# Third convolution tap by an accumulating transfer, and the absolute maximum of four tiles at once on VectorE

## What is computed

```python
def bit_linear(x, w):                       # act_quant: 127 / absmax of a token's row; weight_quant: -1, 0, 1 times a scale
    xq = x + stop_gradient(act_quant(x) - x)
    wq = w + stop_gradient(weight_quant(w) - w)
    return einsum('bsd,hd->bsh', xq, wq)

h = bit_linear(x, w1)                       # 1024 -> 4096
h = depthwise_conv1d(h, conv_w, conv_b)     # three taps along the tokens, padding 1
h = silu(h)
y = bit_linear(h, w2)                       # 4096 -> 1024; needs the absmax of every token over all 4096 rows of h
x = x + layernorm(y)
```

## Time and profile before

| | us |
|---|---|
| median of 3 runs (lowest, highest) | 1610.01 (1600.94, 1643.06) |
| the profiled execution | 1595.02 |
| its span, slowest core (core 3) | 1593.5 |
| spans of the 8 cores | 1575.8 to 1593.5 |
| window 0, from its first scaled copy to the transpose of the maximum | 981.7 to 1099.2 |
| windows 1, 2, 3, the same | 1121.5 to 1225.0; 1257.3 to 1360.0; 1393.0 to 1497.2 |

### The profile page before, as it was taken

The page is one execution under the profiler, slowest core; times in us unless marked ns, Lnnn a source line. Parts: engine busy times, 40 slices in busy tenths (PEclk is TensorE's granted clock), DMA queues, the critical chain, the costliest instruction groups (busy, mean ns, idle before and its releaser), DMA issues.

```text
span 1593.5 us, 23415 instructions; the slowest of 8 cores (1575.8 to 1593.5 us)
## 1 busy us (share of the span) xinstructions
PE 1278.4 (80%) x8148; PEld 794.3 (50%) x8148; DVE 888.0 (56%) x1449; ACT 830.2 (52%) x1118; POOL 94.6 (6%) x165
## 2 busy tenths in 40 slices
PE   2686898798995997988989965653898899799887
...
GB/s 277 194 161 106 179 234 200 188 230 233 172 84 170 154 107 178 153 168 138 187 142 149 146 238 149 166 151 64 1 15 59 61 1 54 41 41 28 27 67 66
DMA packets 86961, 206.31 MB, mean 129 GB/s; under 512 B 8471, under 2 KB 50759, under 8 KB 82668
## 3 DMA queue, kind: packets, MB, share of 16 engines
...
q1 hardware_dynamic: 60620, 91.02, 19.4%
...
HBM read 170.99 MB, written 33.79 MB: 129 GB/s over the span
## 4 chain that ended last, share of the span: by engine, by line
PE 47%; DVE 15%; DMA 13%; issue 11%; ACT 11%; SPq 3%; DVEq 0%; ACTq 0%; POOLq 0%
PE psum L740 11%; PE psum L899 10%; PE psum L863 10%; DMA b_gz<-s_sz 4%; PE psum L653 4%; PE psum L700 4%; DMA f_xr<-x_rev_t 2%; PE psum L800 2%; DMA f_wr<-w_in_t 2%; DMA b_wcb<-w_t 2%; DVE b_h L1357 2%; PE psum L772 2%; DVE b_ev L1309 1%; DVE f_xt L1225 1%; DVE f_xl L1232 1%
## 5 line engine op out<-in xcount | busy, mean ns | idle before, releaser
L863 PE MATMUL psum<-b_xq,b_w1q 128*128 128x257 f16 x2048 | 260.2, 282 | 91.3 <-DVE b_ev L1309 82.6
L863 PEld LDWEIGHTS psum<-b_xq,b_w1q 128*128 128x128 fp8e4 x2048 | 202.2, 101 | 155.2 <-issue 112.9
L899 PE MATMUL psum<-b_w2q,b_hq 128*128 128x512 fp8e4 x1024 | 243.4, 388 | 7.7 <-DVE b_x2t L1394 7.7
L899 PEld LDWEIGHTS psum<-b_w2q,b_hq 128*128 128x128 f16 x1024 | 102.4, 100 | 115.6 <-issue 18.2
L1629 ACT ACTIVATE b_hs<-b_hs,c_cw 128x512 f32<-128x512 f32 x128 | 92.0, 719 | 57.6 <-DVE b_hs L1317 57.5
L1271 DVE SCALAR_TENSOR_TENSOR b_y<-psum,c_dsb,b_gz 128x256 f32<-128x256 f32 (+1 forms) x64 | 30.8, 482 | 147.4 <-PE psum L740 73.0
L1314 DVE SCALAR_TENSOR_TENSOR b_hs<-b_ev,c_cw,b_hs 128x512 f32<-128x512 f32 x128 | 95.1, 743 | 20.6 <-ACT b_hs L1625 20.5
L1317 DVE SCALAR_TENSOR_TENSOR b_hs<-b_ev,c_cw,b_hs 128x512 f32<-128x512 f32 x128 | 96.1, 751 | 14.4 <-DVE b_hs L1314 1.4
L1625 ACT ACTIVATE b_hs<-b_ev,c_cw 128x512 f32<-128x512 f32 x128 | 90.3, 707 | 13.2 <-DVE b_ev L1309 13.2
L1587 ACT ACTIVATE b_yh<-b_y 128x256 bf16<-128x256 f32 (+1 forms) x64 | 26.2, 410 | 129.3 <-DVE b_y L1271 118.0
L1309 DVE TENSOR_TENSOR b_ev<-psum,b_rbc 128x514 f32<-128x514 f32 x128 | 87.4, 685 | 1.0 <-PE psum L863 1.0
...
## 6 DMA issues: line engine op xcount, KB each, us to landing
f_xr<-x_rev_t POOLq DMA_DIRECT2D x15, 2048.0 KB, 11.3
f_pk<-w_t POOLq DMA_DIRECT2D x16, 1024.0 KB, 7.6
b_wca<-w_t POOLq DMA_DIRECT2D x32, 512.0 KB, 4.4
b_wcb<-w_t POOLq DMA_DIRECT2D x32, 512.0 KB, 6.0
b_wck<-w_t POOLq DMA_DIRECT2D x16, 1024.0 KB, 5.0
...
f_lab<-s_logat SPq DMA_DIRECT2D x16, 512.0 KB, 6.5
```

What stands on the lines that cost most here:

```text
L863: e.matmul(psum[:, o:o + 257], sb_w1q.ap()[:, k * DH + mh * 128:k * DH + mh * 128 + 128], x[:, c:c + 257], start=k == 0, stop=k == KD - 1) ...
L899: e.matmul(ps[4 + (t % 2) * 2 + half], sb_hq[i].ap()[:, kh * 128:kh * 128 + 128], sb_w2q.ap()[:, kh * D + half * 512:kh * D + half * 512 + ...
```

## The change

- On most tiles the third tap no longer is a VectorE instruction. ScalarE writes the product of the shifted slot and the third weight to one of two slots of a new buffer `sb_t2` (`tap2`), and GpSimd's queue issues a transfer of that slot, 128 partitions by 2048 bytes (256 KB), that adds it to the tile in `sb_hs` (`accum_op=ALU.add`). `tap_by_dma` says on which: in windows 1 to 3 all tiles below 29, in window 0 the odd ones below 29 (14 of 32).
- A slot of `sb_t2` is used again when the transfer of two users earlier has landed (`TAP`). The scaled copy of a tile waits for `tap2` and the second tap of three tiles earlier, since it overwrites their slot of `sb_ev`.
- SiLU of tile m comes in the loop's step m + 3 and no longer in m + 1, and waits for the transfer, or for `conv`. The last four tiles close up.
- The absolute values on ScalarE (L1637) and the two-tile maxima (L1331) go. VectorE reduces four tiles at once with `tensor_reduce` (maximum of absolute values; the reduced axis steps from tile to tile, 2048 bytes), at g = 8, 12, ... 32, then two tiles at g = 33 and two at g = 34, and takes the maximum with the 512 running columns after each but the first.
- The loads of the second weight matrix move into a loop with the tap transfers on GpSimd's queue.

```diff
+    def tap_by_dma(w, mh):
+        return mh < KH - 3 and (w > 0 or mh % 2 == 1)
...
+                if w or g > 2:
+                    pw, pm = divmod(w * KH + g - 3, KH)
+                    if tap_by_dma(pw, pm):
+                        e.wait_ge(*F_A.at("tap2", pw, pm))
+                    e.wait_ge(*F_V.at("tap1" if tap_by_dma(pw, pm) else "conv", pw, pm))
                 e.tensor_tensor(ev_of(w, g), psum[:, b * 512 + 255:b * 512 + 255 + WX], sb_rbc.ap(), op=ALU.mult
                                 ).then_inc(*F_V.up("ev", w, g))
...
-                                       op0=ALU.mult, op1=ALU.add).then_inc(*F_V.up())
-                e.wait_ge(*F_V.last())
-                e.scalar_tensor_tensor(hs_of(m), x[:, 2:2 + WT], cwb[:, m * 3 + 2:m * 3 + 3], hs_of(m),
-                                       op0=ALU.mult, op1=ALU.add).then_inc(*F_V.up("conv", w, m))
-            if g >= 4 and g % 2 == 0:
-                m = g - 4
-                v_acc(e, w, m)
-        v_acc(e, w, KH - 2)
+                                       op0=ALU.mult, op1=ALU.add).then_inc(*F_V.up("tap1", w, m))
+                if not tap_by_dma(w, m):
+                    e.wait_ge(*F_V.last())
+                    e.scalar_tensor_tensor(hs_of(m), x[:, 2:2 + WT], cwb[:, m * 3 + 2:m * 3 + 3], hs_of(m),
+                                           op0=ALU.mult, op1=ALU.add).then_inc(*F_V.up("conv", w, m))
+            if g >= 8 and g % 4 == 0:
+                v_absmax(e, w, g - 8, 4)
+            if g > KH:
+                v_absmax(e, w, KH - 4 + (g - KH - 1) * 2, 2)
+
+    def v_absmax(e, w, m, n):
+        acc, new = sb_acc.ap()[:, 0:WT], sb_acc.ap()[:, WT:2 * WT]
+        e.wait_ge(*F_A.at("silu", w, m + n - 1))
         if m:
             e.wait_ge(*F_V.last())
-            e.tensor_tensor(sb_acc.ap(), sb_acc.ap(), sb_abs.ap(), op=ALU.max).then_inc(*F_V.up("max", w, m))
+        e.tensor_reduce(new if m else acc, caps(sb_hs, m * WT, [[KH * WT, 128], [1, WT], [WT, n]]), axis=AXX, op=ALU.max,
+                        apply_absolute_value=True).then_inc(*F_V.up())
+        if m:
+            e.wait_ge(*F_V.last())
+            e.tensor_tensor(acc, acc, new, op=ALU.max).then_inc(*F_V.up("acc", w))
...
+                if tap_by_dma(w, g):
+                    if w == 0 and g == 1:
+                        e.wait_ge(*XQST.end())
+                    if tap_same_slot(w, g):
+                        e.wait_ge(*TAP[tap_slot(w, g)].at(*tap_same_slot(w, g)))
+                    e.activation(t2_of(w, g), ev_of(w, g)[:, 2:2 + WT], AF.Copy, scale=cwb[:, g * 3 + 2:g * 3 + 3]
+                                 ).then_inc(*F_A.up("tap2", w, g))
+            for m in range(g - 3, g - 2) if g < KH - 1 else range(g - 3 + (g - KH + 1), g - 1 + (g - KH + 1)):
+                if m >= 0:
+                    a_silu(e, w, m)
+
+    def a_silu(e, w, m):
+        e.wait_ge(*(TAP[tap_slot(w, m)].at(w, m) if tap_by_dma(w, m) else F_V.at("conv", w, m)))
+        e.activation(hs_of(m), hs_of(m), AF.Silu, bias=cwb[:, 96 + m:97 + m]).then_inc(*F_A.up("silu", w, m))
...
+        for w in range(4):
+            for mh in range(KH):
+                if w == 0 and mh % 2 == 0 and mh // 2 + 2 < NCK:
+                    g_w2(e, mh // 2 + 2)
+                if tap_by_dma(w, mh):
+                    e.wait_ge(*F_A.at("tap2", w, mh))
+                    e.wait_ge(*F_V.at("tap1", w, mh))
+                    e.dma_start(out=hs_of(mh), in_=t2_of(w, mh), accum_op=ALU.add).then_inc(*TAP[tap_slot(w, mh)].dma(w, mh))
```

More of the change, by code:

```diff
@@ L278, in write_program @@
     sb_x2t = at("b_x2t", [128, 2 * D], F32, 2 * D * 4)
-    sb_abs = at("b_abs", [128, 2 * WT], F32, 2 * WT * 4)
+    sb_t2 = at("b_t2", [128, 2 * WT], F32, 2 * WT * 4)
     sb_h8 = at("b_h8", [128, 2 * KH * 128], I8, 2 * KH * 128)
@@ L371, in write_program @@
     F_T, F_V, F_A = sig("ffn1_tensor"), sig("ffn1_vector"), sig("ffn1_scalar")
+    TAP = [sig("tap_added0"), sig("tap_added1")]
     K_T, K_V, K_A = sig("hquant_tensor"), sig("hquant_vector"), sig("hquant_scalar")
@@ L1284, in ev_of, with tap_users, tap_slot, tap_same_slot @@
         return sb_ev.ap()[:, o:o + WX]
+    def tap_by_dma(w, mh):
+        return mh < KH - 3 and (w > 0 or mh % 2 == 1)
+    def tap_users(w):
+        return [mh for mh in range(KH) if tap_by_dma(w, mh)]
+    def tap_slot(w, mh):
+        return (sum(len(tap_users(v)) for v in range(w)) + tap_users(w).index(mh)) % 2
+    def tap_same_slot(w, mh):
+        every = [(v, m) for v in range(4) for m in tap_users(v)]
+        i = every.index((w, mh))
+        return every[i - 2] if i > 1 else None
+    def t2_of(w, mh):
+        o = tap_slot(w, mh) * WT
+        return sb_t2.ap()[:, o:o + WT]
     def hs_of(mh, n=1):
@@ L1726, in gpsimd, with g_w2 @@
             e.wait_ge(*X2ST[k].end())
-        for c in range(NCK):
-            if c > 1:
-                e.wait_ge(*QW_A.at("tern2", c - 2))
-            e.dma_start(out=wck_of(c), in_=d_w2[:, c * 2048:c * 2048 + 2048]).then_inc(*W2LD[c % 2].dma(c))
+        for c in range(2):
+            g_w2(e, c)
+        for w in range(4):
[6 more added lines that the diff above has]
+                    e.dma_start(out=hs_of(mh), in_=t2_of(w, mh), accum_op=ALU.add).then_inc(*TAP[tap_slot(w, mh)].dma(w, mh))
+    def g_w2(e, c):
+        if c > 1:
+            e.wait_ge(*QW_A.at("tern2", c - 2))
+        e.dma_start(out=wck_of(c), in_=d_w2[:, c * 2048:c * 2048 + 2048]).then_inc(*W2LD[c % 2].dma(c))
     with nc.Block() as block:
```

17 lines of the change are left out of this document (removed).

## The result

The changed kernel takes 1642.1 us (median of 4 runs, 1639.3 to 1669.9) against 1623.2 us of the kernel before beside it (4 runs, 1600.9 to 1643.1). The ratio of the two is 1.022, interval 1.015 to 1.030: slower by some 35 us of 1600. The forecast was +34 us. (In some executions of either kernel the cores of one die show a lower granted clock and the time is some per cent longer, which raises the medians; the ratios here leave such executions out, and where a profile has such a die I use the other four cores.)

The account below looks back on a forecast made before the run. VectorE was taken to bound the kernel, with TensorE close behind in windows 1 to 3. Window 0 at +11.5 and three others at +7.6 gave +34 us: 1595.0 to 1629, plus 15 for the median, 1644; range 1626 to 1662, 8 in 10 1592 to 1685.

Parts of the forecast that it names:

- the forecast's own: Case with the four-tile reduction near 3.9 us and the transfer from 2.5 to 4.5: +16 to +52 us; chance 0.38.
- its two chains: Window 0: through ScalarE's first tap, 15.0 us a four-tile block against 13.52; other windows: through the transfer, 12.4 against 11.12.
- the longer end of a window: After the last third tap VectorE still has one four-tile and two two-tile reductions with maxima: 11.3 us, +4.5 a window.
- the time given back around the statistics: Windows 1 to 3, around g = 22 to 24: the statistics fit into VectorE's spare time, -4.7 us a window.
- two-tile reduction: VectorE's reduction of two tiles at a window's end, given the strided penalty: 2.04 us instead of 1.23.
- R: Duration of VectorE's four-tile reduction: 3.93 us at the strided rate of 1.84 ns an element, other end 2.29.
- 5.0 + R + T: Windows 1 to 3, chain of a four-tile block through second tap, transfer, `tap2`, first tap and reduction: 12.4 us.
- T: Time of one accumulating tap transfer from issue to landing: 3.5 us, range 2.2 to 6.0.
- VectorE's 9.9 us in a block of 12.4: Windows 1 to 3: VectorE's own steps in a four-tile block, leaving room for the statistics to fit in.
- Unit steps: Rival: the four-tile reduction runs at the unit-step rate, 2.29 us; sum -14 us, so 1596; chance 0.32.
- The slow transfer: Rival: the tap transfer takes 5 us or more; +61 us (1671) at 5, +79 (1689) at 6; chance 0.30.
- TensorE's margin: Windows 1 to 3 before: TensorE less than 6% behind VectorE, so relief of VectorE worth at most 0.66 us in four tiles.

Follow-up runs that it names:

- experiment 4: Changed kernel with other access patterns in its 28 larger reductions: four for one output, 2048 read, takes 2.28 us at step 1, 3.52 at step 4, 3.72 at 512.
- experiment 1: Changed kernel with each reduction reading neighbouring elements at step 1 (wrong groups): reduction 2.28 to 2.29 us, stage 512.0 us against 554.1, ratio to before 0.998.
- experiment 3: Changed kernel with four more slots for the scaled copies of the third tap, from tile 6 of each window on: stage 540.1 us against 554.1, ratio to before 1.014.
- experiment 9: Changed kernel with every tap transfer a plain copy instead of an addition: transfer 2.3 us against 3.4, stage 540.9 us against 554.1.
- experiments 5 to 8: Changed kernel, ratios to before: two-tile maximum 0.995; that with four more slots 0.995; that without transfers 1.017; transfers with the maximum of before 1.005.

## Why the prediction was right

**The total.** +34 forecast; +40 in the stage, some +35 by the ratio of the runs; 1644 against 1642.1. The case that came true is the forecast's own: its two chains and the longer end of a window are in the rows, and only the time given back around the statistics is not. That 1644 is so near is luck in part. It was 1595.0 + 34 + 15, the 15 being what the median of the runs lay above the profiled execution before. After, the median lies 1.5 us below the profiled 1643.6, which is 48.6 above 1595.0: 40 by the change and the rest from outside the stage. The sizes:

| term | forecast | measured |
|---|---|---|
| four-tile reduction | 3.93 us (other end 2.29) | 3.70 |
| two-tile reduction | 2.04 | 1.23 |
| transfer, issue to landing | 3.5 (2.2 to 6.0) | 3.4 |
| block, window 0 | 15.0 | 14.77 (the first 13.97, the last 13.83) |
| block, windows 1 to 3, ahead of the statistics | 12.4 | 12.65 (12.1 to 13.9) |
| block behind the statistics | 12.4 | 13.2 (12.8 to 14.4) |
| window's end, against before | +4.5 | +2.8 |
| given back around the statistics | -4.7 | -0.9 |
| window 0; each other window | +11.5; +7.6 | +8.4; +10.8 |

**The reduction.** Taking the price of L1192 and L1194 was right and L1162 was rightly left aside as a short one-input instruction. The rate I took (1.84 ns an element) is that of a pure stride; with neighbours read along it is 1.73, so R was 0.23 too high. That a one-input reduction would pay the price of a two-input operation was assumed when it was taken; experiment 4 shows it.

**The two-tile reduction** is the term that I had wrong in kind: I gave it the penalty of the four-tile one. It has none. This is most of the window's end: 9.6 us in window 1 (last third tap at 1239.80, end of the fold at 1249.39) against 6.75 of the earlier trace rows, where 11.3 had been forecast. 2 x (2.04 - 1.23) = 1.6 and R's 0.23 account for the difference of 1.7 to within 0.2.

```profile
1239.80 0.75 DVE L1345 SCALAR_TENSOR_TENSOR b_hs<-b_ev,c_cw,b_hs 128x512 f32<-128x512 f32 x1
1240.66 3.68 DVE L1358 TENSOR_REDUCE b_acc<-b_hs 128x512 f32<-128x2048 f32 x1
...
1249.54 1.08 PE L879 MATMUL psum<-c_id,b_acc 128*128 128x128 f32 x4 [5.31 <-DVE b_acc L1362]
```

TensorE's wait before the transpose grew only from 4.65 to 5.31: the fold is later, but TensorE's own work before it is later too.

**The block of windows 1 to 3.** The chain 5.0 + R + T was the right one, and its result right to 0.2 us through three errors that cancel: R 0.23 too high, T 0.1 too high, and GpSimd's 0.55 us between the second tap's end (1192.58) and the issue (1193.13), which I had left out. With all three: 5.0 + 3.70 + 3.4 + 0.5 = 12.6. Experiments 1, 3 and 9 each moved one term: R down by 1.41 took 1.4 off the block, and T down by 1.1 took 0.8 to 1.0, as the slots did, since both end at the loop through TensorE (11.6 and 11.8). That loop is only 1 us below the chain, and the prediction doesn't have it. Many blocks are longer than the chain gives, up to 13.9; no run took that apart.

**Given back around the statistics.** This step failed. The stretch with g = 22 takes 16.42 us (1199.42 to 1215.84), 3.8 over a block, where it was 4.7 over one before. I had argued that VectorE's 9.9 us in a block of 12.4 leave room for them. The rows show why not:

```profile
1204.45 0.74 DVE L1341 SCALAR_TENSOR_TENSOR b_hs<-b_ev,c_cw,b_hs 128x512 f32<-128x512 f32 x1
1205.12 1.29 DVE L1410 BATCH_NORM_STATS2 t_sc<-psum 128x6 f32<-128x512 f32 x2
...
1207.44 0.69 DVE L1336 TENSOR_TENSOR b_ev<-psum,b_rbc 128x514 f32<-128x514 f32 x1
1207.45 1.28 ACT L1705 ACT_TABLE_LOAD   x1 [0.86 <-DVE t_sc L1418]
...
1210.92 0.70 ACT L1656 ACTIVATE b_hs<-b_ev,c_cw 128x512 f32<-128x512 f32 x1
...
1211.73 0.75 DVE L1341 SCALAR_TENSOR_TENSOR b_hs<-b_ev,c_cw,b_hs 128x512 f32<-128x512 f32 x1 [2.33 <-ACT b_hs L1656]
```

The statistics stand right behind the reduction and its second tap, in the part of the block where VectorE has no gap. ScalarE's part waits for them: a table load of 1.28 us at 1207.45, three short conversions and one of 1.15 us, and only behind these comes the first tap, for which VectorE stands 2.33 us. Then VectorE adds the finished tile (1212.39) ahead of its next copy. That is a chain of its own, with R in it and no transfer: the stretch is 16.4 us in experiments 3 and 9 too, and 15.00, 1.4 less, with R at unit rate. The gaps of a block are at its other end, where VectorE waits for TensorE and ScalarE. An engine's spare time in a loop that a chain sets helps only the work that is placed in it. Behind this stretch stands a second cost that I had at nothing: the next block takes 13.2 us, 0.6 over the chain's 12.6 and 1.6 over the 11.55 that it takes in experiment 3 at full clock.

**Windows added up.** Means over the eight cores, against the kernel before. Window 0: from the maximum at g = 8 to that at g = 32 the time is 87.2 us against 80.0, so +7.2; the window's end is +2.8, and the first tiles, ahead of g = 8, are -1.4. Each other window: from g = 8 to g = 32 it is 80.1 against 70.7, +9.4, where the forecast had 7.8 - 4.7 = +3.1; the end is +2.8 for +4.5, and the first tiles are -1.6, for which the forecast had no term. So the total was nearer than it deserved: +11.5 was 3 too high and 3 x 7.6 was 10 too low. In windows 1 to 3 a give-back that was 3.8 too large and blocks longer than the chain gives were met in part by an end 1.7 too long and by the first tiles. The give-back is the largest of these errors.

**The rivals.** *Unit steps* was false for R, and experiment 1 built its world: its window 0 came out as forecast (-2.5 against -2), but the other windows at +0.3 each, not -4, because of the same give-back that didn't come and since the block stayed at 11.2, which is both the chain (5.0 + 2.29 + 3.4 + 0.5) and, but for 0.1, TensorE's pace, and not under 11.1. So the time in that case would have been near before's, not 1596. *The slow transfer* was false, T being 3.4; experiment 9 shows the addition to cost 1.1, so the fear had a cause but not the size. GpSimd's queue behind its loads held nothing up that I could find: its rows name the taps and ScalarE as releasers, and no load.

**TensorE's margin.** I had put relief of VectorE at no more than 0.66 us in four tiles. It is 0.04: 5.54 us a pair against 5.56. The gap of 0.33 us that the earlier trace rows shows is one in the weight loads, which run beside the matmuls, and the matmuls of the pair shown under experiments 5 to 8 had none. The row to read was the matmuls' own timeline.
